# A post-norm transformer layer on one core: a head's turns on TensorE moved behind the unit's turns, and side work's turns held back to the first half of a unit

## The chip, the core and the metric

The kernel runs on one core of one Trainium2 chip, as one program with one launch. The metric is the device time of an execution in microseconds; the number for a kernel is the median over its timed runs. All engines of the core take part: TensorE (PE) multiplies, ScalarE (ACT) and VectorE (DVE) empty its PSUM banks, GpSimd (POOL) scales rows, and SyncE (SP) issues the DMAs.

## The reference, cut to what matters

The input x is 4 sequences of 512 tokens with 512 features. The layer is attention with 16 heads of 32 features (causal, with ALiBi slopes), a residual and a layer norm, then a mixture of 4 experts of which each token uses one, a residual and a layer norm.

```python
q, k, v = split_heads(x @ Wq + bq), split_heads(x @ Wk + bk), split_heads(x @ Wv + bv)
attn = einsum('bhqd,bhkd->bhqk', q, k) / sqrt(32) + alibi
p = softmax(where(causal, attn, finfo(float32).min))
out = einsum('bhqk,bhkd->bhqd', p, v).transpose(0, 2, 1, 3).reshape(4, 512, 512)
x = layernorm(x + out @ Wo + bo)
probs = softmax(x @ Wr + br);  top_w, top_idx = top_k(probs, 1)
y = (silu(x @ Wg[top_idx]) * (x @ Wu[top_idx])) @ Wd[top_idx] * top_w
x = layernorm(x + y)
```

Everything is float32 to the outside. Inside, each large product is made of three products of split operands (a high part in fp32r and a low part that holds what is left).

## The kernel before

Attention is cut into **units**: 4 batches x 16 heads x 3 units, so 192 units, numbered u = 0 to 191. A unit holds the query tiles (3), (0, 1) or (2) of a head, in this order, so u mod 3 says which it is. Four heads make a **group** of 12 units (16 groups, g = 0 to 15; a unit's place in its group is its step), four groups make a batch.

A unit passes through the engines in a software pipeline that every engine runs with the same loop index u: scores of unit u on PE (L698), mask, ALiBi and row maximum on DVE (L1158, `probs`, `neg_max`), the exponential on ACT (L918), the **turns** of unit u-2 on PE (L709: transposes of `probs` against an identity matrix, plain fp32), their high part on ACT (L927, `pT_hi`) and low part on DVE (L1167, `pT_lo`), and then the products with the values of unit u-4 on PE (L726). When a head's three units are through, the head is finished: ACT copies the accumulated bank to `pvT` (L933), PE turns it with 4 small transposes (L735, the **head's turns**, `head_values`), ACT copies their high half (L940, `pv_hi`), DVE makes the inverse row sum and the sum `pv_sum` (L1175, L1176), and POOL writes the head's output to `o_tok` (L1451). The bank in which a head's products accumulate is one of two, so the first product of a head's first unit waits for the `pv_sum` of the head two before it (`s_pvsum`).

Between these pieces PE does **side work**, whose order a planner (`make_plan`) writes out before the program is built. Side jobs are: `xT` (turns of the next batch's x, L615), `K`, `Q` and `V` (projections, L588), `OT` (turns of the finished head outputs, L658), `OP` (the output projection, L588), `x1t` (turns of the normalised rows, L678), and `logit` (L686). Each job has a cost in the planner, and a unit has two halves: half 0 stands between the unit's turns and the products with the values, half 1 behind these. In each half the planner hands out a share of what is owed until the group's end. `ready` holds what a job may rely on. `flush(u)` makes the jobs of the unit before "taken" on ACT and DVE in iteration u, ahead of that iteration's unit work. Two banks serve side jobs in turn.

SP has its own list in program order. In iteration u it first issues, if due, the load of the next batch's x (L472, `x_tok`, 1 MB; due once the last `OP` job of the batch before the last is taken), then a store of normalised rows (L498, `x_scratch`), and then the loads of a head's stacked q and k (L480, six DMAs of a head, `k_stack` and `q_stack`), which wait for the scores of the same head in the group before. K and Q of a group go through one buffer pair (`qk_hi`, `qk_lo`), so ACT's copy of the next K waits until the stack loads of the group before have landed.

The two lines that keep the banks of a head in step on PE are:

```python
if u % PER_HEAD == 0 and hd >= 2:
    pe.wait_ge(s_pvsum, hd - 1)
```

Behind attention come a few routing steps, the gather of rows, and the experts (L810, L822, L835), with the final layer norm at the end. The change doesn't touch them.

## Time and profile before

| | |
|---|---|
| median of 3 runs | 1245.37 us (1242.51 to 1249.0) |
| the profiled execution | 1246.4 us, its span 1244.6 us |
| PE busy | 1163.5 us, 93% of the span |
| DVE, ACT, POOL busy | 768.8, 567.9, 307.7 us |
| mean granted clock of PE | 0.974 |
| chain that ended last | PE 75%, POOL 5%, DVE 5%, ACT 4%, DMA 4%, issue 4% |

The profiled execution is 1.0 us above the median. A busy PE is not a PE at its peak. The span is counted from the first instruction to the last, and the device time has 1.8 us around it.

### The profile page before, as it was taken

The page shows a single profiled execution, that of the slowest core. Times are in us where ns is not written, and L with a number is a line of the kernel's source. Part 1 is how long each engine was busy: PE and PEld are TensorE (multiplying, and loading weights), DVE is VectorE, ACT ScalarE, POOL GpSimd, SP SyncE. Part 2 cuts the span into 40 slices and gives each one's busy share as a digit, 9 for nine tenths or more (in the row PEclk, how much of TensorE's full clock was granted, in tenths as well). Part 3 has the DMA queues.
Part 4 walks back from the last instruction along what each step waited for, and adds up shares of the span by engine and source line. Part 5 has one row for each costly group of instructions (what it writes and reads, how often), then busy time and mean ns, then how long its engine had stood idle before and what let it go on. Part 6 is the DMA issues. An engine that isn't in the chain of part 4 may idle for free.

```text
span 1244.6 us, 27816 instructions
## 1 busy us (share of the span) xinstructions
PE 1163.5 (93%) x8697; PEld 1060.8 (85%) x8697; DVE 768.8 (62%) x1978; ACT 567.9 (46%) x1395; POOL 307.7 (25%) x443
## 2 busy tenths in 40 slices
PE   6998999999999986499999999999999999999994
PEld 5887888888898875498899899889989988998993
DVE  3666778677767775456545664664566366546664
ACT  3676766676767672143232332333233233323354
POOL 5400211201020123433302320331133033113336
PEclk9999999999999997599999999999999999999997
DMA  8222224222322230352223132222312231331202
GB/s 274 65 51 66 68 73 117 53 54 77 94 63 75 67 105 34 109 154 60 77 69 103 48 90 68 69 69 84 88 52 85 69 85 53 88 83 52 86 36 101
DMA packets 109685, 100.11 MB, mean 80 GB/s; under 512 B 12847, under 2 KB 81839, under 8 KB 109552
## 3 DMA queue, kind: packets, MB, share of 16 engines
q1 hardware_dynamic: 104784, 87.85, 25.0%
q0 software_dynamic: 3040, 9.18, 2.2%
q8 instruction: 84, 1.38, 0.5%
q10 hardware_dynamic: 1728, 1.31, 0.3%
q14 instruction: 49, 0.40, 0.1%
HBM read 64.74 MB, written 9.18 MB: 59 GB/s over the span
## 4 chain that ended last, share of the span: by engine, by line
PE 75%; POOL 5%; DVE 5%; ACT 4%; DMA 4%; issue 4%; SPq 2%; ACTq 0%; DVEq 0%; POOLq 0%
PE bank L810 35%; PE bank L588 13%; PE bank L835 10%; PE bank L726 4%; PE bank L709 4%; POOL up_lo L1460 4%; PE bank L822 3%; PE bank L698 2%; SPq L480 2%; DMA up_raw<-in_Wu_dram 2%; DMA q_stack<-qk_lo 1%; ACT probs L918 1%; DVE probs L1158 1%; PE bank L735 1%; PE bank L686 1%
## 5 line engine op out<-in xcount | busy, mean ns | idle before, releaser
L810 PE MATMUL bank<-up_hi,xsT_hi 128*128 x1216 | 355.9, 293 | 6.9 <-POOL up_lo L1460 5.6
L810 PE MATMUL bank<-up_hi,xsT_lo 128*128 x1216 | 344.2, 283 | 0.0
L810 PE MATMUL bank<-up_lo,xsT_hi 128*128 x1216 | 344.2, 283 | 0.0
L1460 POOL TENSOR_TENSOR up_lo<-up_raw,up_hi 128x256 fp32r<-128x256 f32 x241 | 169.7, 741 | 479.4 <-ACT up_hi L950 479.2
L1299 DVE SCALAR_TENSOR_TENSOR h_tok<-bank,row_weight,silu 128x128 f32<-128x128 f32 x304 | 93.5, 347 | 292.5 <-ACT silu L1014 291.3
L810 PEld LDWEIGHTS bank<-up_hi,xsT_hi 128*128 128x128 f32 x1216 | 232.6, 191 | 13.5 <-issue 13.2
L810 PEld LDWEIGHTS bank<-up_hi,xsT_lo 128*128 128x128 f32 x1216 | 233.4, 192 | 0.3
L810 PEld LDWEIGHTS bank<-up_lo,xsT_hi 128*128 128x128 f32 x1216 | 232.8, 191 | 0.0
L1014 ACT ACTIVATE silu<-bank 128x256 f32<-128x256 f32 (+1 forms) x160 | 59.6, 373 | 364.1 <-PE bank L810 364.1
L1316 DVE TENSOR_TENSOR y<-bank,y 128x512 f32<-128x512 f32 x295 | 199.0, 689 | 0.4
L918 ACT ACTIVATE probs<-probs,neg_max 128x512 f32<-128x512 f32 (+3 forms) x256 | 136.5, 558 | 59.9 <-DVE neg_max L1158 58.9
L1158 DVE CUSTOM_DVE_ANT_0 probs<-bank,dist 128x512 f32<-128x512 f32 (+3 forms) x256 | 119.3, 485 | 25.5 <-PE bank L698 24.7
L927 ACT ACTIVATE pT_hi<-bank 128x384 fp32r<-128x384 f32 (+1 forms) x192 | 99.8, 520 | 58.7 <-PE bank L709 58.3
L1167 DVE TENSOR_TENSOR pT_lo<-bank,pT_hi 128x384 fp32r<-128x384 f32 (+1 forms) x192 | 114.5, 597 | 19.0 <-ACT pT_hi L927 18.6
L835 PE MATMUL bank<-down_hi,hT_hi 128*128 x304 | 124.2, 409 | 1.3 <-DVE y L1316 0.6
L950 ACT ACTIVATE up_hi<-up_raw 128x256 fp32r<-128x256 f32 x256 | 85.4, 407 | 84.5 <-DMA up_raw<-in_Wu_dram 84.5
L835 PE MATMUL bank<-down_lo,hT_hi 128*128 x304 | 119.2, 392 | 0.0
L835 PE MATMUL bank<-down_hi,hT_lo 128*128 x304 | 119.0, 392 | 0.0
L726 PE MATMUL bank<-pT_hi,v 128*65 128x128 f32 x640 | 102.0, 231 | 6.1 <-DVE pv_sum L1176 6.0
L1451 POOL TENSOR_TENSOR o_tok<-pv_sum,row_inv 128x128 f32<-128x128 f32 x64 | 25.6, 400 | 331.5 <-DVE pv_sum L1176 320.2
L709 PE MATMUL bank<-ident,probs 128*128 128x128 f32 x640 | 102.4, 274 | 1.9 <-ACT probs L918 0.9
L726 PE MATMUL bank<-pT_lo,v 128*65 128x128 f32 x640 | 97.6, 224 | 0.0
(168 smaller groups left out, 2081.9 us busy)
## 6 DMA issues: line engine op xcount, KB each, us to landing
up_raw<-in_Wg_dram SPq DMA_DIRECT2D x64, 256.0 KB, 3.6
up_raw<-in_Wu_dram SPq DMA_DIRECT2D x64, 256.0 KB, 4.4
down_raw<-in_Wd_dram SPq DMA_DIRECT2D x64, 256.0 KB
k_stack<-qk_hi SPq DMA_DIRECT2D x128, 64.0 KB, 2.0
q_stack<-qk_hi SPq DMA_DIRECT2D x128, 64.0 KB, 2.0
k_stack<-qk_lo SPq DMA_DIRECT2D x64, 64.0 KB, 2.0
q_stack<-qk_lo SPq DMA_DIRECT2D x64, 64.0 KB, 2.0
x_tok<-in_x_dram SPq DMA_DIRECT2D x3, 1024.0 KB, 6.5
```

The costliest lines, as they stand in the source:

```text
L588: mm = pe.matmul(bank_ap, a(k), b(k), start=(i == 0), stop=(i == len(steps) - 1))
L709: mm = pe.transpose(bank[:, j * P:(j + 1) * P], probs[:, u % NP, j * P:(j + 1) * P], ident[:, :])
L726: mm = pe.matmul(bank[0:VW, i * P:(i + 1) * P], v[:, g // 2 % 2, j, g % 2 * GH + h, :], part[:, u % NP, at + j * P:at + (j + 1) * P], star ...
L810: mm = pe.matmul(bank[:, n * 2 * P:(n + 1) * 2 * P], a[:, s, k, :], up_w[w][k][:, :, :].rearrange("p a f -> p (a f)")[:, bass.ds(at, 2 * P ...
L835: mm = pe.matmul(bank[:, :], a[:, s, :], down_w[w][:, :, :].rearrange("p a f -> p (a f)")[:, bass.ds(at, D)], start=(q == 0), stop=(q == 2))
L918: ex = act.activation(probs[:, u % NP, at:at + width], probs[:, u % NP, at:at + width], ACT.Exp, scale=-1.0, bias=neg_max[:, u % NP, i:i + 1])
L927: act.activation(pT_hi[:, u % NP, 0:blocks * P], banks[2 + u % 2][:, 0:blocks * P], ACT.Copy).then_inc(s_pThi, 1)
L1158: bi = dve.tensor_tensor_reduce(out=probs[:, u % NP, at:at + width], in0=banks[u % 2][:, at:at + width], in1=dist[:, SEQ - width:SEQ], sca ...
L1167: dve.tensor_tensor(pT_lo[:, u % NP, 0:blocks * P], banks[2 + u % 2][:, 0:blocks * P], pT_hi[:, u % NP, 0:blocks * P].bitcast(F32), ALU.su ...
L1299: hh = dve.scalar_tensor_tensor(h_tok[:, idx % 2, n, :], gu[:, n, 1, :], row_weight[:, s:s + 1], silu[:, idx % 2, n, :], ALU.mult, ALU.mult)
L1316: dve.tensor_tensor(y[:, s, :], banks[D_BANKS[idx % 3]][:, :], y[:, s, :], ALU.add).then_inc(s_y, 1)
L1460: pool.tensor_tensor(up_w[1][k][:, e, :], up_raw[:, idx % NUPS, k, :, :].rearrange("p g f -> p (g f)"), up_w[0][k][:, e, :].bitcast(F32), ...
```

## The change

Four edits, all in attention.

1. On PE the head's turns are issued in the same iteration as before, but right behind the turns of unit u-2, ahead of half 0 and of the products with the values; before they stood behind these products and ahead of half 1.
2. On ACT, DVE and POOL `head_values` runs one iteration sooner (condition `u - VLAG - 1` in place of `u - VLAG - 2`). On DVE it stands now behind `unit_transposed` and no longer ahead of it.
3. The planner counts a head's output as ready one unit sooner.
4. The planner starts no `xT`, `OT` or `x1t` job in half 1, except in the last 6 units. Such a job then waits for the next half 0, and what is queued behind it waits too.

```diff
@@ -166,6 +166,9 @@
         while budget > 0 and (left or queue):
             if not left:
+
+                if half and queue[0][0] in ("xT", "OT", "x1t") and u < U - PER_GROUP // 2:
+                    return
                 if any(k not in ready for k in needs(queue[0])):
                     return
@@ -231,8 +234,8 @@
             work(u, 0, owed() / (PER_GROUP - step))
-        if u > VLAG + PER_HEAD + 2 and (u - VLAG - 3) % PER_HEAD == 0:
-            ready.add(("o", (u - VLAG - 3) // PER_HEAD - 1))
+        if u > VLAG + PER_HEAD + 1 and (u - VLAG - 2) % PER_HEAD == 0:
+            ready.add(("o", (u - VLAG - 2) // PER_HEAD - 1))
@@ -742,13 +745,13 @@  (tensor)
                 if 2 <= u < U + 2:
                     unit_transpose(u - 2)
+                if u > VLAG + PER_HEAD and (u - VLAG - 1) % PER_HEAD == 0:
+                    head_values((u - VLAG - 1) // PER_HEAD - 1)
                 if u < U:
                     for job, i0, i1 in plan.slices[u, 0]:
                         side(job, i0, i1)
                 if u >= VLAG:
                     unit_values(u - VLAG)
-                    if u > VLAG + PER_HEAD and (u - VLAG - 1) % PER_HEAD == 0:
-                        head_values((u - VLAG - 1) // PER_HEAD - 1)
@@ -975,8 +978,8 @@  (scalar; the same edit in gpsimd)
-                if u > VLAG + PER_HEAD + 1 and (u - VLAG - 2) % PER_HEAD == 0:
-                    head_values((u - VLAG - 2) // PER_HEAD - 1)
+                if u > VLAG + PER_HEAD and (u - VLAG - 1) % PER_HEAD == 0:
+                    head_values((u - VLAG - 1) // PER_HEAD - 1)
@@ -1194,10 +1197,10 @@  (vector)
                 if u < U:
                     unit_biased(u)
-                if u > VLAG + PER_HEAD + 1 and (u - VLAG - 2) % PER_HEAD == 0:
-                    head_values((u - VLAG - 2) // PER_HEAD - 1)
                 if 2 <= u < U + 2:
                     unit_transposed(u - 2)
+                if u > VLAG + PER_HEAD and (u - VLAG - 1) % PER_HEAD == 0:
+                    head_values((u - VLAG - 1) // PER_HEAD - 1)
```

The changed kernel has three lines more at the top, so L588 of before is L591 there, and so on.

**Place 1, TensorE, unit 29 (group 2).** The rows before: scores (L698), the unit's turns (L709), a product of the job `Q` in half 0 (L588), the products with the values (L726), the head's turns (L735), and the product of half 1.

```order
441 L698 MATMUL bank<-k_stack,q_stack 128x384
442 L709 MATMUL bank<-ident,probs 128x128 x4
443 L588 MATMUL bank<-xT_hi,w_hi_72 128x512
444 L726 MATMUL bank<-pT_hi,v 65x128
445 L726 MATMUL bank<-pT_lo,v 65x128
446 L726 MATMUL bank<-pT_hi,v 65x128
447 L726 MATMUL bank<-pT_lo,v 65x128
448 L726 MATMUL bank<-pT_hi,v 65x128
449 L726 MATMUL bank<-pT_lo,v 65x128
450 L735 MATMUL bank<-ident,pvT 128x65 x4
451 L588 MATMUL bank<-xT_hi,w_lo_75 128x512
```

And in the changed kernel:

```order
441 L701 MATMUL bank<-k_stack,q_stack 128x384
442 L712 MATMUL bank<-ident,probs 128x128 x4
443 L738 MATMUL bank<-ident,pvT 128x65 x4
444 L591 MATMUL bank<-xT_hi,w_hi_72 128x512
445 L729 MATMUL bank<-pT_hi,v 65x128
446 L729 MATMUL bank<-pT_lo,v 65x128
447 L729 MATMUL bank<-pT_hi,v 65x128
448 L729 MATMUL bank<-pT_lo,v 65x128
449 L729 MATMUL bank<-pT_hi,v 65x128
450 L729 MATMUL bank<-pT_lo,v 65x128
451 L591 MATMUL bank<-xT_hi,w_lo_75 128x512
```

The four transposes went from behind the products with the values to behind the unit's turns. Over the whole of attention the places at which a run of turns begins behind something that isn't one fall from 276 to 197. Of the 64 head's turns 34 had a product (L588) behind them, 21 the next scores.

**Place 2, VectorE, units 26 to 28.** Before: the low part of unit 24's turns, the taking of job K of group 3 (L1107), then scores of unit 27 (L1158), and behind them the head's reciprocal and sum (L1175, L1176).

```order
123 L1167 TENSOR_TENSOR pT_lo<-bank,pT_hi 128x512
124 L1107 SCALAR_TENSOR_TENSOR qk_lo<-bank,bias_col,qk_hi 128x512
125 L1158 ISA probs,neg_max<-bank,dist 128x512
126 L1158 ISA neg_max 128x1
127 L1175 RECIPROCAL row_inv<-pv_hi 128x4
128 L1176 TENSOR_TENSOR pv_sum<-bank,pv_hi 128x128
129 L1167 TENSOR_TENSOR pT_lo<-bank,pT_hi 128x384
```

In the changed kernel:

```order
123 L1170 TENSOR_TENSOR pT_lo<-bank,pT_hi 128x512
124 L1178 RECIPROCAL row_inv<-pv_hi 128x4
125 L1179 TENSOR_TENSOR pv_sum<-bank,pv_hi 128x128
126 L1110 SCALAR_TENSOR_TENSOR qk_lo<-bank,bias_col,qk_hi 128x512
127 L1161 ISA probs,neg_max<-bank,dist 128x512
128 L1161 ISA neg_max 128x1
129 L1170 TENSOR_TENSOR pT_lo<-bank,pT_hi 128x384
```

The head's pair moved ahead of the taking of K, and no `pT_lo` waits behind it any more.

**Place 3, SyncE, units 77 to 83 (group 6).** The load of x for batch 2 and the stack loads around it. Before:

```order
138 L480 DMA q_stack<-qk_lo 32x512
139 L472 DMA x_tok<-in_x_dram 128x4x512
140 L480 DMA k_stack<-qk_hi 32x512 x2
141 L480 DMA k_stack<-qk_lo 32x512
142 L480 DMA q_stack<-qk_hi 32x512 x2
143 L480 DMA q_stack<-qk_lo 32x512
144 L498 DMA x_scratch<-res 128x512
```

In the changed kernel:

```order
139 L501 DMA x_scratch<-res 128x512
140 L483 DMA k_stack<-qk_hi 32x512 x2
141 L483 DMA k_stack<-qk_lo 32x512
142 L483 DMA q_stack<-qk_hi 32x512 x2
143 L483 DMA q_stack<-qk_lo 32x512
144 L475 DMA x_tok<-in_x_dram 128x4x512
145 L501 DMA x_scratch<-res 128x512
```

The x load moved behind the six loads of one head, because its last `OP` job (row tile 3) is taken in iteration 81 and no longer in 80; the stack loads of iteration 80 wait for the scores of unit 80. It is the same in group 10 for batch 3. The planner's slices around it, in words: the job `OT` of row tile 3 and the `OP` of row tile 2 (in half 1 of unit 71 before) come at units 75 to 76, K and Q of group 7 at 72 to 74 in front of them, and the logit job of row tile 2 and the `x1t` of row tile 3 (units 82) fall into group 7 (92 to 94). Units 85 and 87 are left without side work, and 86 has the second pair of `xT` jobs (before: half 1 of 85); the first product of K of group 8 stands in unit 88 and no longer in 87.

## Rows read from the trace of the kernel before

**Rows 1.** Windows: length, busy of PE, PEld, DVE, ACT, POOL; clock, DMA, GB/s.

```profile
29.50:467.50 438.00, 420.40 (x3527) 374.97 (x3528) 317.85 (x984) 303.13 (x661) 69.54 (x118) 0.99 0.28 74
87.50:90.90 3.40, 3.40 (x22) 3.01 (x21) 2.02 (x9) 2.63 (x7) 0.15 (x1) 0.50 0.00 0
213.50:222.30 8.80, 6.75 (x63) 5.65 (x61) 6.97 (x19) 6.91 (x15) 0.40 (x1) 1.00 0.30 87
```

**Rows 2.** Waits of PE in attention: us in total, times, longest.

```profile
PE bank L726 <- DVE pv_sum L1176: 5.5, 9, 2.1
PE bank L588 <- DVE xT_lo L1100: 2.3, 3, 0.8
PE bank L615 <- DVE xT_lo L1100: 1.9, 3, 0.8
PE bank L686 <- DVE x1T_lo L1131: 1.2, 3, 0.5
```

**Rows 3.** Timeline of units 28 and 29: start, duration, engine, line.

```profile
84.76 0.69 ACT L893 ACTIVATE qk_hi<-bank,bias_col 128x512 fp32r<-128x512 f32 x1 [2.82 <-DMA q_stack<-qk_lo]
86.15 0.68 DVE L1158 CUSTOM_DVE_ANT_0 probs<-bank,dist 128x512 f32<-128x512 f32 x1
87.25 0.25 PE L726 MATMUL bank<-pT_hi,v 128*65 128x128 f32 x1 [2.12 <-DVE pv_sum L1176]
88.49 0.52 PE L698 MATMUL bank<-k_stack,q_stack 96*128 96x384 f32 x1
```

**Rows 4.** Groups of ACT in attention: count, busy us, mean ns, idle before.

```profile
L918 ACT ACTIVATE probs<-probs,neg_max 128x512 f32<-128x512 f32 (+3 forms) x256 | 136.5, 558 | 59.9 <-DVE neg_max L1158 58.9
L927 ACT ACTIVATE pT_hi<-bank 128x512 fp32r<-128x512 f32 x190 | 98.9, 520 | 56.8 <-PE bank L709 56.4
L933 ACT ACTIVATE pvT<-bank 65x512 f32<-65x512 f32 x62 | 36.3, 585 | 0.0
L940 ACT ACTIVATE pv_hi<-bank 128x132 f32<-128x132 f32 x61 | 16.7, 274 | 0.0
```

**Rows 5.** Window of units 178 to 187: where side work is thin.

```profile
436.00:454.00 18.00, 14.51 (x145) 12.84 (x145) 14.19 (x53) 16.50 (x42) 7.15 (x12) 1.00 0.58 171
```

**Rows 6.** Timeline of PE: turns ahead of products, head's turns alone, turns behind turns.

```profile
106.97 0.60 PE L709 MATMUL bank<-ident,probs 128*128 128x128 f32 x4
107.33 0.30 PE L726 MATMUL bank<-pT_hi,v 128*65 128x128 f32 x1
...
117.69 0.43 PE L735 MATMUL bank<-ident,pvT 65*128 65x65 f32 x4
117.92 0.36 PE L588 MATMUL bank<-w_hi,xT_hi 128*128 128x256 f32 x1
118.12 0.28 PE L588 MATMUL bank<-w_hi,xT_lo 128*128 128x256 f32 x1
...
213.88 0.49 PE L709 MATMUL bank<-ident,probs 128*128 128x128 f32 x3
214.21 1.19 PE L615 MATMUL bank<-ident,x_tok 128*128 128x128 f32 x8
```

**Rows 7.** Timeline of PE: a product behind the products with the values.

```profile
120.59 0.33 PE L588 MATMUL bank<-w_lo,xT_hi 128*128 128x256 f32 x1
120.76 0.28 PE L588 MATMUL bank<-w_hi,xT_hi 128*128 128x256 f32 x1
```

**Rows 8.** The x load of batch 2 on SP, and its time to landing.

```profile
207.51 0.58 SPq L472 DMA_DIRECT2D x_tok<-in_x_dram  x1
...
211.28 0.59 SPq L480 DMA_DIRECT2D q_stack<-qk_lo  x1
...
DMA to landing us min/median/max: 6.5/6.5/6.5
```

**Rows 9.** Timeline of PE: the first product of K of group 8.

```profile
222.28 0.47 PE L588 MATMUL bank<-xT_hi,w_hi 128*128 128x512 f32 x1 [0.76 <-DVE xT_lo L1100]
```

**Rows 10.** Timeline of PE: the first product of batch 3's OP job, unit 188.

```profile
456.19 0.47 PE L588 MATMUL bank<-w_hi,oT_hi 128*128 128x512 f32 x1 [0.32 <-DVE oT_lo L1120]
```

More of the change, by code:

```diff
@@ L1470, in gpsimd @@
                     split_up(0, step // 2)
-                if u > VLAG + PER_HEAD + 1 and (u - VLAG - 2) % PER_HEAD == 0:
-                    head_values((u - VLAG - 2) // PER_HEAD - 1)
+                if u > VLAG + PER_HEAD and (u - VLAG - 1) % PER_HEAD == 0:
+                    head_values((u - VLAG - 1) // PER_HEAD - 1)
                 if u < U and step == PER_GROUP - 1 and g % GPB == GPB - 1 and g + 1 < NG:
```

## The prediction

> **What bounds the kernel now.** I read four views. First the windows: attention takes 438.0 us of the span, and PE is busy in 420.4 us of them at a granted clock of 0.99 [rows 1]. The experts behind it aren't touched by the change, so all that it can win or lose lies in these 438 us, and at most 17.6 us of them are idle time of PE. DVE has 317.9 and ACT 303.1 us there [rows 1]: neither is full as a mean.
>
> Second, the waits of PE there [rows 2]. The largest entry is the wait of a head's first product for `pv_sum`, 5.5 us in 9 waits; then waits for the low part of `xT` (2.3 + 1.9 us) and for `x1t` (1.2). The change speaks to each of these.
>
> Third, the groups of ACT [rows 4]: a head costs ACT 4 exponentials at 558 ns, 3 copies at 520, one at 585 and one at 274, so 4.65 us, or 1.55 us per unit. A unit of 438.0/192 = 2.28 us has room for that; a unit with no side work, some 1.2 us of PE, has not. So there are two kinds of stretches. Where side work is thick, PE is the limit, and ACT and DVE wait for it. Where it is thin, ACT is: in the 18 us around units 178 to 187 ACT is busy in 16.50, PE in 14.51 [rows 5]. A wait taken from PE in a thin stretch comes back as another unless ACT or DVE really gets work sooner. This decides how much of the 17.6 us can be had.
>
> Fourth, single places in the timeline, for which see below.
>
> **Part 1: the head's turns in another place on PE.** The number of transposes is the same; only what stands next to them differs. Alone, behind the products with the values, the four take 0.23 us to the start of the next product (117.69 to 117.92), and this product takes 0.20 us to the next start [rows 6], against 0.17 for one directly behind the products with the values [rows 7]: 0.26 us in all. Behind the unit's turns the price must be put together. A turn that is followed by a turn takes 0.11 us (three in 213.88 to 214.21), but the last one of a run only some 0.03: four of them ahead of a product take 0.36 us (106.97 to 107.33) [rows 6]. What a run saves at its end it pays in the product behind it, so one long run is not cheaper than two. In the new place the unit's last turn takes its full 0.11 us, and the added four cost 0.08 + 0.23 = 0.31 us. For a head with a product behind it that is 0.05 us worse, with scores behind it about as much better. The sum over 64 heads is anywhere from -3 to +3 us, and I take 0. The 27 runs of side turns that leave the second halves (31 to 4) are costed by the same rows at 0, within 1 us.
>
> **Part 2: `pv_sum` one iteration sooner.** The largest of the waits, 2.12 us, is at unit 28 [rows 3]. There ACT's taking of K waited 2.82 us for stack loads and ran at 84.76; DVE, behind it, had the scores of unit 27 ready at 86.15 + 0.68 = 86.83, and after that the `pv_sum` for which PE stood until 87.25. The next scores came at 88.49. In the changed order `pv_sum` is ahead of the taking of K (place 2), so PE does the products with the values and one product (0.7 us) inside the stall and is then held by the scores buffer, which is free at 86.83. So the next scores come up to 88.49 - 86.83 = 1.66 us sooner. Behind the 2.12 us of idle time the granted clock was 0.50 for 3.40 us [rows 1]. With two shorter pauses in its place the clock may stay up, which is worth at most 3.40/2 = 1.70 us, and less since DVE is also behind there: I take 0.6. Together 2.2 us, with bounds of 1.0 and 3.4.
>
> The other 3.4 us of `pv_sum` waits [rows 2] are nearly all in thin stretches. By the share that ACT has there (92% busy, [rows 5]) most of it comes back as a wait for ACT. Two of them lie in the stretch of part 3, which I cost as a whole. For the rest I take 1.0 us, with bounds of 0 and 2.5. On DVE `pT_lo` no longer stands behind the head's pair (262 ns and the reciprocal), which helps the same places and isn't counted again. ACT's `pv_hi` now stands ahead of the exponential of u mod 3 = 2 and pushes it by 0.27 us [rows 4]; and PE asks for `pvT` earlier by half 0 and the products with the values, which in a thin unit leaves ACT 1.2 us for a copy and `pvT`, 0.52 + 0.59 = 1.11 us [rows 4]. The price is 0.3 us in all, bound 2.
>
> **Part 3: side turns only in first halves.** Here whole jobs move. In group 7 (and 11) K started at 222.28 after 0.76 us of wait for `xT`, in unit 87 [rows 9]; from the first scores of unit 84 (213.5) to there PE was busy 6.75 of 8.8 us, DVE 6.97 and ACT 6.91 [rows 1]. The change puts the second pair of x turns in unit 86 and K in unit 88, so K comes one whole unit later in the order, while the two waits for `xT` and one for `pv_sum` have a unit more of ACT and DVE work to lie in. A unit more is 1.55 us of ACT against 0.76 + 0.82 + 0.47 us of waits that go away: about even, the unit's work itself not being lost. In group 3 it is the same.
>
> What is new there is the load of x (place 3). Before it was issued at 207.51 and landed 6.5 us later, at 214.0, and the turns that need it began at 214.21 [rows 6, 8]: 0.2 us to spare. Now six stack loads stand ahead of it, which take 3.8 us of SP (from the end of its own issue at 208.1 to 211.28 + 0.59, [rows 8]), and the first of them waits for the scores of unit 80. Units 72 to 80 come some 0.5 to 3 us sooner, since the side work of a second half of unit 71 is now spread over group 6, and the first thin unit is 81 as before. I expect the load at about 209.2 and landed at 215.7, and PE there at 213 to 214: a wait of about 2 us. Most of it is not lost, as ACT and DVE are the limit in units 81 to 88 and use it: I charge 0.5 us for each of the two groups, with bounds of 0 and 3.8. The Trainium skill (DMA: Bandwidth & Descriptors, "Anatomy of one DMA — SWDGE (gpsimd) path") gives a DMA as 2.0 us plus bytes over 436 GB/s, so as an estimate 4.4 us for this 1 MB. The trace says 6.5 us [rows 8], with stack loads beside it on the same engines, and decides. By the page the load would land about when PE comes, and the sum would be 1.0 us lower.
>
> The logit job that waited for `x1t` in unit 82 (and 130) moved to group 7 (and 11) into thick units, which removes up to two of the three waits that make 1.2 us [rows 2]; and the `OT` job of unit 58 (and 106) no longer asks for the bank of `V` in the unit in which `V` is taken. Both are thin places, and I take 0.6 us together, bounds 0 and 2.
>
> **Part 4: outputs ready one unit sooner.** Only the last batch gains: its first turns come in unit 186 in place of 187, and the first product in the second half of 187 in place of 188 (456.19, behind 0.32 us of wait, [rows 10]). POOL has the outputs by then, since the head's scaling now stands ahead of a long split. A unit without side work is 1.2 us of PE in a place where PE waits for ACT: I take 0.5 us, bounds 0 and 1.5.
>
> **Sum.** 0 (part 1) - 2.2 - 1.0 + 0.3 (part 2) + 1.0 - 0.6 (part 3) - 0.5 (part 4) = -3.0 us. Against its own execution of 1246.4 us that is 1243.4; the median of before is 1.0 us lower, so I predict 1242.4 us as the median. This kernel's runs lie within 6.5 us of each other, so about 0.5% (6.2 us) is what a measurement can tell from no change.
>
> **The rivals.** *The switch costs more than starts show (faster).* If going from products to turns and back has a price that the rows of starts hide, it falls away at 276 - 197 = 79 places. Between two products the first one behind a run of turns takes 0.20 in place of 0.17 us, and behind the unit's turns (0.31 to the next start) it is nearer to 0.1 us over; 79 x 0.1 is 8 us, and with the 3 above this gives 1234. For it: such a surplus is there behind each run. Against it: the last turn of a run gives about as much back.
>
> *The x load becomes the wait (slower).* If PE really comes at 213 or sooner and the stretch isn't limited by ACT, each of two groups waits up to 3.8 us, and behind each the clock may fall as it did behind 2.12 us (3.40 us at 0.50, so 1.7 us more). That is 2 x 5.5 = 11.0 us in place of the 1.0 charged, and with the other parts' -4.0 it gives +7.0 us, 1252. It decides from a wait of about 2.5 us in each. For it: the 0.2 us to spare before. Against it: ACT's load between the same units.
>
> *Nothing comes of it.* PE's waits at unit 28 and in the thin stretches come back one instruction later, because ACT and DVE are behind, not `pv_sum`: 1245.
>
> **How the numbers follow.** The forecast as it stands, a gain of 1 to 6 us, gets 0.55. The dear switch gets 0.19 and lies beyond 0.5%. The x load gets 0.14, of which 0.06 is beyond 0.5%. No effect gets 0.12. So faster 0.19, same 0.75 (0.55 + 0.08 + 0.12), slower 0.06. Bounds of the parts: the gains of part 2 run from 1.0 to 5.9, part 1 adds 3 either way, part 3 up to 6.6 more. The range of 1237 to 1249 leaves out most of the dear switch and the far end of the x load, about 2 in 10.
>
> **What the changed profile would show.** If I am right: the entry "`bank` of the values' products <- `pv_sum`" falls from 5.5 us to under 1.5; no half clock at about 87 us; units 28 to 31 are some 2 us shorter; at about 213 us PE waits 1 to 3 us for `x_tok`, and again 110 us later; waits for `pvT` grow to 1 or 2 us; attention ends about 3 us sooner and the experts' time is unchanged. The prediction is wrong if products behind turns take other times than now, if the clock falls at the x waits, or if the idle time in attention stays at 17.6 us although `pv_sum` has gone from the list.

## The result: slower by 0.4%, and the profile after

The changed kernel takes 1250.17 us (median of 6 runs, 1247.84 to 1252.97), the kernel before 1244.56 in the same comparison (6 runs, 1242.51 to 1249.0). The ratio is 1.0044, 95% interval 1.0028 to 1.0060: 5.6 us slower, where I had forecast 3 us faster. The time lies 1.2 us above my range.

The profiled execution took 1252.97 us with a span of 1251.2. First the windows of the changed kernel (columns as in rows 1): attention, three stretches in which the clock fell, and three stretches of units, 60 to 95, 108 to 143 and 180 to 190.

```profile
28.10:470.30 442.20, 422.19 (x3527) 378.18 (x3528) 316.70 (x986) 304.32 (x662) 71.25 (x119) 0.99 0.28 73
29.20:32.60 3.40, 3.40 (x10) 2.63 (x9) 0.69 (x6) 1.42 (x3) 3.37 (x2) 0.50 0.38 96
213.50:216.90 3.40, 3.33 (x18) 3.36 (x19) 1.42 (x3) 1.20 (x2) 0.00 (x0) 0.50 0.04 11
329.50:332.90 3.40, 3.40 (x25) 3.40 (x23) 2.08 (x7) 1.87 (x4) 0.00 (x0) 0.51 0.10 28
150.56:243.16 92.60, 87.10 (x716) 78.44 (x714) 65.24 (x198) 60.20 (x130) 8.15 (x20) 0.98 0.28 78
267.68:358.17 90.49, 86.94 (x715) 78.39 (x714) 65.46 (x198) 59.87 (x129) 8.12 (x20) 0.98 0.28 77
441.88:468.15 26.27, 22.31 (x188) 19.07 (x186) 18.23 (x59) 19.74 (x49) 7.14 (x12) 1.00 0.26 74
```

The same three stretches of units in the kernel before:

```profile
154.91:243.84 88.93, 86.36 (x725) 77.22 (x722) 66.23 (x199) 59.31 (x129) 9.81 (x22) 1.00 0.29 80
267.66:356.64 88.98, 86.35 (x724) 77.19 (x722) 66.31 (x199) 59.48 (x129) 9.76 (x22) 1.00 0.29 80
439.72:465.28 25.56, 22.18 (x188) 19.27 (x186) 18.20 (x59) 19.48 (x49) 7.15 (x12) 1.00 0.31 93
```

Attention took 442.2 us in place of 438.0 [rows 1], and the place of the loss is plain: units 60 to 95 and 108 to 143 took 183.1 us together in place of 177.9, so 5.2 us more. PE's idle time in them, the length less PE's busy time, grew from 5.2 to 9.05 us, and 6.8 us of them ran at half clock, where before none did. In the changed kernel the stretches even hold a little less work: the last logit job of the batch (8 small products, about 0.9 us) comes behind unit 95. The rest of attention differs by -1.0 us: the half clock at 87.5 us that [rows 1] shows isn't in this execution, and the tail (units 180 to 190) is 0.7 us longer. Of the span's other 2.4 us, 1.4 less lie ahead of attention, 0.2 more in the routing, and 3.5 more in the experts, whose code is the same. Half of that is a half-clock stretch at 756 us, and other kernels below had the experts up to 3 us shorter than before, so I count it as scatter.

Now PE's waits in attention (us in total, times, longest):

```profile
PE bank L618 <- DMA x_tok<-in_x_dram: 6.5, 2, 3.8
PE bank L738 <- ACT pvT L936: 3.3, 8, 1.4
PE bank L712 <- ACT probs L921: 1.9, 8, 0.3
PE bank L591 <- DVE xT_lo L1103: 1.8, 3, 1.1
PE bank L701 <- DVE neg_max L1161: 1.1, 2, 0.8
PE bank L661 <- POOL o_tok L1454: 1.0, 1, 1.0
```

The 5.5 us for `pv_sum` [rows 2] are gone, as the change means to do. At the top stands a wait that wasn't there, for the x load, in units 84 and 132. The SP queue's timeline, and PE's at the same place:

```profile
205.45 0.59 SPq L483 DMA_DIRECT2D q_stack<-qk_lo  x1
206.09 0.58 SPq L475 DMA_DIRECT2D x_tok<-in_x_dram  x1
```

```profile
208.99 0.45 PE L701 MATMUL bank<-k_stack,q_stack 96*128 96x512 f32 x1
213.57 1.94 PE L618 MATMUL bank<-ident,x_tok 128*128 128x128 f32 x8 [3.80 <-DMA x_tok<-in_x_dram]
...
221.99 0.47 PE L591 MATMUL bank<-xT_hi,w_hi 128*128 128x512 f32 x1 [0.44 <-DVE xT_lo L1103]
```

What ACT and DVE did meanwhile is seen in two windows, PE's wait in unit 84 and its wait in unit 132, and in DVE's first instruction behind the first of them:

```profile
209.77:213.57 3.80, 0.00 (x1) 0.03 (x1) 2.83 (x9) 2.06 (x5) 0.40 (x1) 0.99 0.89 302
326.29:328.96 2.67, 0.00 (x0) 0.03 (x1) 2.67 (x9) 1.61 (x5) 0.40 (x1) 1.00 1.01 345
```

```profile
215.32 0.69 DVE L1103 TENSOR_TENSOR xT_lo<-bank,xT_hi 128x512 fp32r<-128x512 f32 x1 [2.72 <-ACT xT_hi L884]
```

DVE had work for the whole of the shorter wait, and for 2.83 us of the longer one; then it stood idle for 2.72 us until the x turns had come through PE and ACT.

The load is issued behind the stack loads at 206.09, not later than before on the clock (207.51, [rows 8]). But PE asks for it at 213.57 - 3.80 = 209.77, 3.7 us behind the issue, where it came 6.7 us behind it before (214.21, [rows 6]). The clock times of the two executions can't be compared directly, as unit 60 starts at 150.56 here and at 154.91 before. Counted from there, PE asks when it did (59.2 us behind it, before 59.3), and the load goes out 2.9 us later (55.5 against 52.6); it also takes longer, 7.3 us to landing (before 6.5) and 7.5 to PE's start. PE waits 3.80 us; right at its end the clock falls for 3.40 us (the eight turns take 1.94 us in place of 1.19). In unit 132 the same happens with 2.67 us. So K of group 8 starts 221.99 - 150.56 = 71.4 us behind the first scores of unit 60; before it was 222.28 - 154.91 = 67.4.

### The profile page after: what moved, and what is told of

Its sections match the earlier page's. It is cut to its first block, busy times and chain, and to the rows that moved or that the text cites. A ratio compares the mean times of both kernels' runs of the same rounds, so it can differ in the third digit from the quotient of the medians.

```text
span 1251.2 us, 27816 instructions
## 1 busy us (share of the span) xinstructions
PE 1166.8 (93%) x8697; PEld 1065.8 (85%) x8697; DVE 767.6 (61%) x1978; ACT 568.8 (45%) x1395; POOL 305.9 (24%) x443
## 4 chain that ended last, share of the span: by engine, by line
PE 77%; DMA 4%; POOL 4%; DVE 4%; issue 4%; ACT 4%; SPq 3%; ACTq 0%; DVEq 0%; POOLq 0%
PE bank L813 35%; PE bank L591 13%; PE bank L838 11%; PE bank L729 4%; PE bank L712 4%; POOL up_lo L1463 3%; PE bank L825 3%; PE bank L701 2%; SPq L483 2%; DMA up_raw<-in_Wu_dram 2%; DMA x_tok<-in_x_dram 2%; PE bank L689 1%; DMA q_stack<-qk_lo 1%; PE bank L738 1%; ACT probs L921 1%
```

## The experiments

All are timed beside the kernel before. In the text, "the two stretches" are units 60 to 95 and 108 to 143, 177.9 us together in the kernel before. "Edits" are: 1 PE's order, 2 the order on ACT, DVE and POOL, 3 the planner's `ready` for outputs one unit sooner, 4 the rule for second halves.

**Edits 1 to 3 without the rule.**

```
-                if half and queue[0][0] in ("xT", "OT", "x1t") and u < U - PER_GROUP // 2:
-                    return
```

> Edits 1 to 3 without edit 4: the head's turns, copy, sum and output sooner, side turns allowed in both halves as before. If the loss of the changed kernel (5.6 us on the medians) comes from edit 4, this one is faster than before: the wait for pv_sum at unit 28 and the half clock behind it go away, some 2 to 4 us, so 1240.5 to 1242.5. If the loss comes from the head's part (PE asks for pvT too early; 3.8 us of such waits in the changed kernel), this one is slower than before, 1246 or more. No wait for x_tok is expected.

Measured: 1246.43 us, ratio 1.0015 (1.0000 to 1.0030). The moved head saves nothing; by the interval it costs between 0 and 4 us.

**The rule alone, on the kernel before.**

```
+                if half and queue[0][0] in ("xT", "OT", "x1t") and u < U - PER_GROUP // 2:
+                    return
```

> Edit 4 alone (side turns only in first halves), the head's part as before. If edit 4 carries the loss and the head's part gains, this is the slowest of all: 5.6 us plus the 2 to 4 us that the head's part gives, so 1252 to 1254, with the waits for x_tok of 2.5 us or more at units 84 and 132. If the parts don't add up (the head's part is neutral), 1250.

Measured: 1251.13 us, 1.0050 (1.0032 to 1.0067), with 6.2 us of waits for `x_tok` and 183.3 us for the two stretches. The rule by itself brings the whole loss. The time is near the 1250 us that I expected of a neutral head's part, not the 1252 to 1254 of one that gains.

**The changed kernel, x load one SP iteration sooner**, so ahead of the six stack loads.

```
-                if ... plan.flushed.get(("OP", (x_due - 2) * QT + QT - 1), U + 9) <= u:
+                if ... plan.flushed.get(("OP", (x_due - 2) * QT + QT - 1), U + 9) <= u + (x_due < NB):
```

> The changed kernel, with one difference: SP issues the load of x one iteration sooner, ahead of the six stack loads of that head, as the kernel before had it. If the late load is the loss: the two waits for x_tok (6.5 us together) and the half clock behind them (2 times 3.4 us at 0.50) go away, up to 9 us of it if nothing else limits, at least 4: 1241 to 1246. If ACT and DVE were the limit there anyway and the planner's thin units are the loss: 1249 to 1250.

Measured: 1248.11 us, 1.0029 (1.0013 to 1.0044). PE's waits for the load halve:

```profile
PE bank L618 <- DMA x_tok<-in_x_dram: 3.1, 2, 1.9
```

The two stretches fall to 179.5 us. This lies between my two expectations. By the medians the load's place on SP makes up some 2 of the 5.6 us, but the two intervals overlap, so this isn't clear of noise. The load still waits for the last OP job of its batch, which the rule has put one iteration later.

**Edit 1 alone: only PE's order.**

```
+                if u > VLAG + PER_HEAD and (u - VLAG - 1) % PER_HEAD == 0:
+                    head_values((u - VLAG - 1) // PER_HEAD - 1)
                 if u < U:
                     for job, i0, i1 in plan.slices[u, 0]:
...
-                    if u > VLAG + PER_HEAD and (u - VLAG - 1) % PER_HEAD == 0:
-                        head_values((u - VLAG - 1) // PER_HEAD - 1)
```

> Before, with edit 1 alone: the head's turns behind the unit's turns on PE; copy, sum and output keep their old iteration on ACT, DVE and POOL. This is the price of the neighbourhood of turns by itself, with the earlier demand for pvT, and without the sooner pv_sum. If the switch between products and turns is dear (0.1 us at each of 64 places): 1238 to 1240. If a run's end gives back what the product behind it takes, as the rows of before say: 1244 to 1246. If the waits for pvT decide: 1246 to 1248.

Measured: 1245.58 us, 1.0012 (0.9996 to 1.0028); the two stretches 178.2 us. What stands next to a run of turns costs nothing that these runs can tell. The waits for `pv_sum` stay, at unit 28 too (first the list of waits, then PE's timeline):

```profile
PE bank L726 <- DVE pv_sum L1176: 5.5, 10, 1.6
```

```profile
85.59 0.25 PE L726 MATMUL bank<-pT_hi,v 128*65 128x128 f32 x1 [1.60 <-DVE pv_sum L1176]
```

and yet units 28 and 29 took 5.15 us, against 7.2 before: no half clock followed in this execution. Nor did one in the kernel with only the x load moved (below), whose instructions here are those of the kernel before:

```profile
88.66 0.25 PE L726 MATMUL bank<-pT_hi,v 128*65 128x128 f32 x1 [1.92 <-DVE pv_sum L1176]
```

**Edits 2 and 3 alone: the other engines sooner, PE's turns in their old place.** The diff is that of the change for ACT, DVE, POOL and `ready`, without PE's four lines.

> Before with edits 2 and 3 alone: ACT, DVE and POOL do the head's copy, sum and output one iteration sooner, but PE keeps the head's turns behind the products with the values. Theory that the 1.5 us of the head's part (e1_heads_only) come from PE asking for pvT too early: those waits stay at the 0.7 us of before, pv_sum waits are gone, 1243 to 1245. Rival, that it is ACT's copy pv_hi ahead of the exponential: ACT now waits for turns that come later still, 1247 or more. If neither matters: 1245 to 1246.

Measured: 1252.44 us, 1.0061 (1.0043 to 1.0079), the slowest of all. Its waits:

```profile
PE bank L615 <- DVE xT_lo L1100: 3.5, 2, 1.7
...
PE bank L698 <- DVE neg_max L1158: 3.2, 4, 1.1
PE bank L658 <- DVE v L1111: 3.0, 3, 1.4
```

ACT's `pv_hi` stands ahead of an exponential here, and its turns come late on PE, so the exponential and all behind it wait. ACT's own waits show it; before, `pv_hi` waited for nothing [rows 4]:

```profile
ACT pv_hi L940 <- PE bank L735: 14.2, 21, 1.1
```

Edit 2 needs edit 1. The reverse doesn't hold: edit 1 alone costs no more than both.

**The rule for x turns only**, with edits 1 to 3.

```
-                if half and queue[0][0] in ("xT", "OT", "x1t") and u < U - PER_GROUP // 2:
+                if half and queue[0][0] in ("xT",) and u < U - PER_GROUP // 2:
```

> The changed kernel with edit 4 for the xT jobs alone; OT and x1t may start in half 1. The last OP job of a batch keeps its old place, so the x load isn't late. If the late load and the moved OT jobs are the loss: about e1_heads_only plus 0 to 1 us, 1246 to 1247.5, no wait for x_tok. If the two empty units around the second pair of xT jobs cost: 1248 to 1250.

Measured: 1245.20 us, 1.0016 (1.0001 to 1.0030), as without the rule. K of group 8 is in unit 88, one unit later than before, and costs nothing.

**The rule for OT and x1t turns only.** The same line with `("OT", "x1t")`.

> The changed kernel with edit 4 for OT and x1t alone; xT may start in half 1. The load of x is late as in the changed kernel, with waits of 2.5 to 4 us for x_tok at units 84 and 132. If these are the loss: 1249.5 to 1251, all of the changed kernel's. If the empty units around xT are a part of it: 1247.5 to 1249.

Measured: 1251.33 us, 1.0057 (1.0040 to 1.0075), 6.7 us of waits for `x_tok`. The loss sits in this part of the rule.

This kernel's profile (1247.45 us, 3.9 below its median) gives a pair of places that differ in the clock alone, but for K's unit. In unit 132 PE waits for x as long as in the changed kernel (2.66 against 2.67 us), and here the clock stays up. Shown are PE's line, and then windows of units 108 to 143, of the wait, and of the 3.40 us behind it:

```profile
328.63 1.06 PE L618 MATMUL bank<-ident,x_tok 128*128 128x128 f32 x8 [2.66 <-DMA x_tok<-in_x_dram]
```

```profile
267.37:356.79 89.42, 85.41 (x715) 76.70 (x714) 65.20 (x198) 59.51 (x129) 8.12 (x20) 1.00 0.29 77
325.97:328.63 2.66, 0.00 (x1) 0.03 (x1) 2.66 (x9) 1.60 (x5) 0.40 (x1) 1.00 0.96 343
328.63:332.03 3.40, 3.40 (x36) 3.40 (x37) 2.27 (x8) 2.74 (x6) 0.00 (x0) 1.00 0.23 75
```

The units take 89.4 us where the changed kernel's take 90.5; of the difference some 0.2 us is K one unit later (89.45 us with edits 1 to 3, 89.65 with the rule for x turns too). In its unit 84 this kernel waits 4.01 us, the clock falls for 6.80 us, and units 60 to 95 take 92.9.

**The kernel before, with the x load one SP iteration later** and nothing else: the same line as above with `<= u - (x_due < NB)`.

> Before, with one difference: SP issues the load of x one iteration later, behind the six stack loads of a head (3.8 us). Nothing else moves. It measures the price of a late load by itself. The load had 0.2 us to spare, so PE waits about 3.5 us at unit 84 and again at 132. If nothing gives it back: 7 us, and up to 3.4 us more by half clock, 1252 to 1255. If ACT and DVE were the limit there and use the wait, as the prediction said: 1245.5 to 1247. In between, 2 us for each load, 1248 to 1250, is what the changed kernel against e3_x_early (2.1 us for both) would lead to, with 1247 at the least.

Measured: 1247.71 us, 1.0022 (1.0010 to 1.0034). The late load alone costs about 3 us, half of what the changed kernel loses. The profiled execution took 1253.9, 6 us over that median, so its rows overstate it; they show what a late load can do (a wait, then two windows):

```profile
PE bank L615 <- DMA x_tok<-in_x_dram: 8.0, 2, 4.7
```

```profile
216.80:223.60 6.80, 5.43 (x32) 5.46 (x33) 2.49 (x7) 2.82 (x6) 0.00 (x0) 0.50 0.08 26
332.80:339.60 6.80, 5.63 (x33) 5.66 (x34) 3.29 (x10) 3.63 (x8) 0.40 (x1) 0.50 0.32 118
```

**Edits 1 and 2 alone**: as the first experiment, with `ready` for outputs as before.

```
-        if u > VLAG + PER_HEAD + 1 and (u - VLAG - 2) % PER_HEAD == 0:
-            ready.add(("o", (u - VLAG - 2) // PER_HEAD - 1))
+        if u > VLAG + PER_HEAD + 2 and (u - VLAG - 3) % PER_HEAD == 0:
+            ready.add(("o", (u - VLAG - 3) // PER_HEAD - 1))
```

> Edits 1 and 2 without edits 3 and 4: the head's turns, copy, sum and output are moved as in the changed kernel, but the planner marks a head's output ready where the kernel before did, so the last batch's output turns stay in unit 187 and no slice differs from before. If the longer tail (units 184 to 188, 13.9 us in place of 12.75) is what edit 3 costs, the time is 1.0 to 1.5 us below edits 1 to 3 (1246.4, ratio to before 1.0015), so about 1245.2, ratio 1.0 to 1.0005, and the tail takes 12.6 to 13.0 us. If the tail is longer because pvT is asked for sooner, whatever the planner does, the time stays at 1246 to 1247, ratio 1.001 to 1.002, and the tail at 13.5 to 14.

Measured: 1244.96 us, 1.0011 (0.9995 to 1.0027); units 184 to 188 took 13.2 us, between the two expectations. The timed runs can't tell 1.0011 from 1.0015. The profiles say more. Without edit 3, units 180 to 190 and the two waits in them:

```profile
436.30:462.70 26.40, 22.33 (x188) 18.97 (x187) 18.37 (x59) 19.73 (x49) 7.17 (x12) 1.00 0.29 86
```

```profile
447.52 0.46 PE L735 MATMUL bank<-ident,pvT 65*128 65x65 f32 x4 [1.43 <-ACT pvT L933]
453.61 0.48 PE L588 MATMUL bank<-w_hi,oT_hi 128*128 128x512 f32 x1 [0.87 <-DVE oT_lo L1120]
```

With edit 3 (the first experiment):

```profile
441.28:470.53 29.25, 25.06 (x188) 21.54 (x186) 18.37 (x59) 20.08 (x49) 7.15 (x12) 0.88 0.28 83
454.50:461.30 6.80, 6.01 (x26) 5.47 (x27) 3.36 (x11) 3.52 (x8) 0.40 (x1) 0.50 0.26 77
```

```profile
452.49 0.46 PE L735 MATMUL bank<-ident,pvT 65*128 65x65 f32 x4 [1.42 <-ACT pvT L933]
455.29 1.51 PE L658 MATMUL bank<-ident,o_tok 128*128 128x128 f32 x6 [1.00 <-POOL o_tok L1451]
```

The wait for `pvT` is there with and without edit 3, so it comes from edits 1 and 2. With edit 3 the output turns wait 1.00 us for POOL right behind, and the clock falls. Of the 14 kernels profiled, 9 have edit 3, and 6 of these show half clock between units 184 and 190 (the changed kernel's own profile doesn't); of the 5 without it 1 does.

**The changed kernel with the rule lifted in units 71 and 119**, the two halves that make the x load late.

```
-                if half and queue[0][0] in ("xT", "OT", "x1t") and u < U - PER_GROUP // 2:
+                if half and queue[0][0] in ("xT", "OT", "x1t") and u < U - PER_GROUP // 2 and u not in (71, 119):
```

> The changed kernel with the rule lifted in units 71 and 119 alone. There the OT and OP jobs fill the second half as before, batch 1's last OP job is taken in iteration 80 again, and the x load goes out ahead of the stack loads; 24 of the rule's 27 moves stay, and K of group 8 comes in unit 89, a unit later still than in the changed kernel (88; before 87). If the loss of the changed kernel is the late x load, which these two halves cause, PE waits under 0.5 us for x_tok and the time is 1245.0 to 1247.5, ratio 1.000 to 1.002, 3 to 5 us below the changed kernel. If it is the thinner first halves and the later K that cost, it stays at 1249 to 1252, ratio 1.0035 to 1.006, with no wait for x_tok.

Measured: 1249.28 us, 1.0044 (1.0029 to 1.0060), with no wait for `x_tok` at all. My theory, that the late load is the whole loss, falls here. The two stretches are as long as in the changed kernel, 182.8 us, for another reason:

```profile
149.04:240.69 91.65, 88.18 (x724) 79.07 (x722) 66.62 (x201) 60.56 (x131) 7.98 (x20) 0.98 0.27 76
264.08:355.20 91.12, 87.07 (x723) 77.54 (x722) 66.56 (x201) 60.88 (x131) 7.95 (x20) 1.00 0.28 77
```

Of this, 1.2 us are two new waits of 0.6 us for `oT_lo` in units 60 and 108, behind the moved `OT` jobs; the changed kernel has one of them, in unit 60. For the rest, either K in unit 89, two units late, is the cost, or the new places of the x1t and logit jobs. Two more kernels tell these apart.

**The rule for x1t only** (the same line with `("x1t",)`): x1t and logit jobs in the new places, K in unit 87.

> Edits 1 to 3 with the rule for x1t jobs alone. In groups 6 and 10 the x1t jobs move to first halves (units 77, 81, 83) and the logit job from unit 82 to 83; the OP jobs, and so the x load, stay as before, and K of group 8 stays in unit 87. If what made the kernel with the rule lifted in units 71 and 119 slow is K in unit 89, two units late, this kernel costs what edits 1 to 3 cost: 1245 to 1247, ratio 1.001 to 1.002, and units 60 to 96 and 108 to 144 take at most 1.5 us more than before together. If it is the x1t and logit jobs' new places, the ratio is 1.003 to 1.0045 (1247.5 to 1249.5) and these units take 3 us or more over before.

Measured: 1245.79 us, 1.0019 (1.0000 to 1.0037). The two stretches take 179.9 us, 2.0 over before, a little more than the 1.5 I had allowed; one of them holds a half clock.

```profile
152.94:242.64 89.70, 86.75 (x723) 77.53 (x722) 66.53 (x200) 60.02 (x129) 8.00 (x20) 1.00 0.28 78
266.38:356.55 90.17, 88.00 (x724) 79.01 (x722) 66.62 (x200) 59.93 (x129) 7.97 (x20) 0.98 0.28 78
```

**The rule for xT and x1t** (`("xT", "x1t")`): the same places, but K in unit 89.

> Edits 1 to 3 with the rule for xT and x1t jobs, and not for OT. Each of the two alone leaves K of group 8 in unit 88 or 87; together they push it to 89. The x load is on time. If K two units late is the cost, this is as slow as the kernel with the rule lifted in units 71 and 119, which has the same slices there: 1248 to 1250, ratio 1.0035 to 1.005, with units 60 to 96 and 108 to 144 taking 4 to 5.5 us over before together. If the OT jobs' places cost beside it, it is nearer to 1246.5, ratio 1.002.

Measured: 1249.68 us, 1.0054 (1.0033 to 1.0076).

```profile
153.15:244.10 90.95, 88.18 (x723) 78.98 (x722) 66.63 (x201) 60.65 (x130) 7.97 (x20) 0.98 0.28 76
267.96:358.39 90.43, 87.11 (x723) 77.47 (x722) 66.60 (x201) 60.78 (x130) 7.95 (x20) 1.00 0.28 78
```

```profile
PE bank L738 <- ACT pvT L936: 6.0, 8, 1.4
```

The last row is from its waits in attention. The rule for x turns alone is free, that for x1t turns nearly so, and both together cost as much as the change. So the record points to K two units late, with PE waiting for ACT (6.0 us for `pvT` in attention, against 3.9 with the rule for x1t). It doesn't prove it: the intervals of the two kernels, 1.0000 to 1.0037 and 1.0033 to 1.0076, just touch, and the two stretches take 181.4 us, 3.5 over before, less than the 4 to 5.5 I had expected and half of what the ratio says. The profiled execution is 2.7 us below the median.

All together, ordered by the time from the first scores of unit 60 to K of group 8 (K of group 12 comes up to 3.4 us nearer):

```
kernel                        K in unit  K starts after  waits x_tok  two stretches  ratio
before                        87         67.4 us         0            177.9          1
edit 1 alone                  87         67.4            0            178.2          1.0012
edits 1, 2                    87         67.7            0            178.8          1.0011
edits 1 to 3, rule x1t        87         68.0            0            179.9          1.0019
edits 1 to 3                  87         68.1            0            179.3          1.0015
edits 1 to 3, rule xT         88         69.1            0            179.4          1.0016
changed, x load sooner        88         69.1            3.1          179.5          1.0029
rule alone                    88         70.4            6.2          183.3          1.0050
edits 1 to 3, rule OT, x1t    87         70.6            6.7          182.3          1.0057
changed kernel                88         71.4            6.5          183.1          1.0044
edits 1 to 3, rule xT, x1t    89         71.7            0            181.4          1.0054
before, x load later          87         71.8            8.0          185.4          1.0022
changed, rule lifted at 71    89         72.3            0            182.8          1.0044
```

Up to 69.1 us the ratio is at most 1.003, from 70.4 on at least 1.0044, save for the kernel before with the late load. The ratio is of medians and all else in the table is of one profiled execution each, which lies up to 6 us above the median (x load later 6.2, edits 1 to 3 5.4, x load sooner 4.4) or below it (rule OT, x1t 3.9; edits 1, 2 2.9). It is an order, then, and no measured law. Edits 2 and 3 alone aren't in it: there K starts after 68.3 us and the two stretches take 179.2, so its 1.0061 must come from elsewhere, from its own waits in attention, as far as is known. No kernel beats the one before.

What a pause costs is seen more closely from the moment at which PE asks for x to the first product of K. The unit that holds K counts by itself, so the rows stand in two blocks:

```
kernel, units                          wait x_tok  half clock  asking to K
K in unit 87 or 135
edits 1 to 3, 108 to 143               0           0           8.4 us
edits 1 to 3, 60 to 95                 0           3.4         8.8
rule OT, x1t, 108 to 143               2.7         0           8.6
before, x load later, 108 to 143       3.2         6.8         10.9
rule OT, x1t, 60 to 95                 4.0         6.8         11.4
before, x load later, 60 to 95         4.7         6.8         12.4
K in unit 88 or 136
edits 1 to 3, rule xT, 108 to 143      0           0           9.6
edits 1 to 3, rule xT, 60 to 95        0           3.4         9.8
changed, x load sooner, 108 to 143     1.2         0           9.4
changed, x load sooner, 60 to 95       1.9         3.4         9.9
changed kernel, 108 to 143             2.7         3.4         10.7
rule alone, 60 to 95                   3.2         3.4         11.0
rule alone, 108 to 143                 3.0         6.8         12.0
changed kernel, 60 to 95               3.8         3.4         12.2
```

(The kernel before, in both groups: 8.1. The kernels in which a moved x1t job puts off the asking itself aren't in this table.) A wait of 2.7 us with the clock up puts K off by 0.2 us, and 3.4 us of half clock without a wait for x by 0.2 to 0.4. The two together put it off by 1.2 us at a wait of 2.7 (10.72 less 9.56), and by 2.7 us at a wait of 3.8. No row has a wait of over 2.7 us with the clock up.

## Why the prediction was wrong

**Part 1** was right: 0 was forecast, and edit 1 alone moves the two stretches by 0.3 us. With that the rival of a dear switch is out.

**Part 2** was wrong. I forecast -2.2 us at unit 28, -1.0 elsewhere and +0.3. Edits 1 and 2 give +1.4 (1.0011), not -2.9. The step that failed is "so the next scores come up to 1.66 us sooner", with the 0.6 for the clock. PE's waits in unit 28 of the changed kernel:

```profile
85.89 0.44 PE L701 MATMUL bank<-k_stack,q_stack 96*128 96x384 f32 x1 [0.76 <-DVE neg_max L1161]
86.65 0.66 PE L712 MATMUL bank<-ident,probs 128*128 128x128 f32 x4 [0.31 <-ACT probs L921]
87.51 0.46 PE L738 MATMUL bank<-ident,pvT 65*128 65x65 f32 x4 [0.20 <-ACT pvT L936]
```

They make 1.27 us in place of 2.12, and units 28 and 29 took 5.3 us; but with edit 1 alone, `pv_sum` as late as ever, they took 5.15. In the 13 profiles beside that of before they take 4.7 to 5.6 us, with or without edit 2. Of the 2 us by which the 7.2 of before stand out, 1.7 are the half clock of that one execution, which comes or doesn't. Over attention the 5.5 us for `pv_sum` became 3.3 for `pvT` (before 0.7; I had said 1 to 2), 1.9 for `probs`, 1.1 for `neg_max` and 1.0 for `o_tok`. For this part the rival "nothing comes of it" was right.

**Part 3** decided the result. I placed the x load rightly, behind six stack loads, and forecast a wait of about 2 us; it was 3.80 and 2.67. The step that failed is the charge "most of it is not lost, as ACT and DVE are the limit in units 81 to 88 and use it: I charge 0.5 us for each of the two groups". The two groups took 5.2 us more in place of 1.0. The reason that I gave holds as far as it goes: DVE was busy for all of the wait of 2.67 us, and the other kernel's wait of 2.66 us with the clock up put K off by only 0.2. Two things were missing. The first is the clock, which the sum put at nothing: it fell behind both waits, and wait and half clock together put K off by 1.2 us behind unit 132. The second is the length: at 3.80 us DVE ran out of work after 2.83, and K came 2.7 us late. These 3.9 us are most of the 5.2; 0.6 more are the new wait for `oT_lo` in unit 60, behind the moved `OT` job, which I hadn't seen. The rest isn't split further; edits 1 to 3 by themselves cost 1.4 us in these units.

The wait was sized too low for two reasons. The load took 7.3 us to land, and 7.5 us to PE's start, and not 6.5; and PE asked 3.7 us behind the issue, where my times (issue at 209.2, PE at 213 to 214) gave 3.8 to 4.8. That both came some 3 to 4 us sooner on the clock than I had put them is a shift of the whole stretch, unit 60 included, and no part of it.

"A unit more ... about even" held for K one unit late (1.0016 against 1.0015) and, as it seems, not for two. The gain of 0.6 us for the logit and OT jobs wasn't seen: the rule for x1t alone gives 1.0019. The Trainium skill (DMA: Bandwidth & Descriptors, "Anatomy of one DMA — SWDGE (gpsimd) path") would have the load landed after an estimated 4.4 us and the wait under 1 us. That figure is for DMAs issued from GpSimd, and this load goes out on SP's queue, so it was the wrong one to hold against the trace; PE's turns began 7.5 us behind the issue (206.09 to 213.57).

**Part 4** was wrong in sign: -0.5 forecast, units 180 to 190 took 0.7 us more in the changed kernel's profile and 3.7 more with edits 1 to 3 (6.80 us of half clock among them). I had said that POOL has the outputs by then; PE waits 1.0 us for them.

**The rival of the x load** had it: it gave 1252 us, decided from waits of 2.5 us, and named the fall of the clock behind them. Both waits passed that point and both were followed by 3.40 us at half clock. Its price of 5.5 us a group was too high (1.5 and 3.7 measured). I had given it 0.14, on the strength of ACT's load between the same units. That was a mean over a window (6.91 of 8.8 us), which doesn't say how much work is at hand when PE stops: DVE had 2.83 us of it, ACT 2.06. What speaks for the outcome was in the prediction: 0.2 us to spare, and 3.8 us of stack loads put ahead of the load.

## What to carry over

A wait in a thin stretch is absorbed as far as the neighbouring engines have their input already, here some 2.7 us of it; beyond that it moves the start of the next thick work. Price a change by that start. Count a transfer's slack from the issue to the consumer, and both from a common point ahead of the stretch, since the clock times of two executions are shifted against each other. A half clock behind a wait is chance: don't book its absence as a gain, and don't leave it out of the price of a new wait.

## What the runs showed of the hardware

In attention, stretches at half clock (3.40 us, sometimes 6.80) come at places that change from one profiled execution to another, mostly behind waits of PE. The same place can have one or not: behind 2.12 us of wait in unit 28 before and not behind 1.92 us there in a kernel with the same instructions; behind 2.67 us in unit 132 of the changed kernel, and not behind 2.66 us there with the rule for OT and x1t. In such a stretch a product with the values starts every 0.11 us, and at full clock every 0.06 (kernel before, 90.09 to 90.20 and 92.17 to 92.23 us).

Over all timed runs the mean granted clock was 0.973 to 0.974 for the kernel before, 0.971 for the changed kernel, 0.970 for edits 1 to 3, 0.968 for the rule alone, 0.969 for edits 2 and 3 alone. Taken as time at half clock, 2 x (1 - clock) x span, that is 65 to 68 us before and 73 us after. But the kernel with edits 1 to 3 and the rule for x turns also has 73 us, at a ratio of 1.0016, so more time at half clock doesn't make up the loss by itself. In the second table above it counts where it falls together with a wait on the way to K. How much a wait of 3.8 us would cost with the clock up isn't known: no profiled execution has one.
